# Meta keys' row maxima taken off by one product of 16 rows instead of eight with diagonals, in layer 0's attention

## What is computed

```python
x = L0_attn_x
xn = _layernorm(x, axis=-1)
x = x + _L0_attn_ref(xn, ...) + _L0_ffn_ref(xn, ...)
xn = _layernorm(x, axis=-1)
x = x + _L1_attn_ref(xn, ...) + _L1_ffn_ref(xn, ...)

# in _L0_attn_ref: N_HEADS = 16, N_KV_HEADS = 4, WINDOW = 64, N_META = 16, hd = 16
for qs in range(0, S, WINDOW):
    k_c = jnp.concatenate([k[:, :, :meta_end], k[:, :, ls:qe]], axis=2)
    allowed = causal & (in_window | meta)
    scores = jnp.einsum('bhqd,bhkd->bhqk', q_c, k_c) * scale
    scores = jnp.where(allowed[None, None], scores, -jnp.inf)
    attn = jax.nn.softmax(scores, axis=-1)
    chunks.append(jnp.einsum('bhqk,bhkd->bhqd', attn, v_c))
```

## Time and profile before

| | |
|---|---|
| three runs | 1292.34, 1292.8, 1294.93 us (median 1292.8) |
| profiled execution, its own time | 1302.65 us |
| its span, first to last instruction | 1300.9 us |
| TensorE busy | 1243.3 us, 96% |
| VectorE busy | 706.2 us, 54% |
| ScalarE busy | 576.4 us, 44% |
| GpSimd busy | 728.1 us, 56% |
| mean granted TensorE clock | 0.984 |

### The profile page before, as it was taken

How to read it: one execution, slowest core, us unless ns; L and a number is a source line. 1 busy time by engine, 2 the same in 40 slices (tenths; PEclk the granted TensorE clock), 3 DMA queues, 4 the chain that set the end, 5 groups by cost and what they waited for, 6 DMA issues and landing times. The chain is left out here.

```text
span 1300.9 us, 22025 instructions
## 1 busy us (share of the span) xinstructions
PE 1243.3 (96%) x7969; PEld 1075.5 (83%) x7969; DVE 706.2 (54%) x1449; ACT 576.4 (44%) x1239; POOL 728.1 (56%) x549
## 2 busy tenths in 40 slices
PE   7688999999989998999999999999999999999999
PEld 6467888888857887888788888888888888899988
DVE  6994555555667667675645434434434334554445
ACT  4675566666555333334333334333343333444431
POOL 4646777776203554566666664766556554177620
PEclk9699999999998999999999999999999999999999
DMA  9624888876705111121221112111111102699931
GB/s 314 166 54 108 180 174 189 177 172 128 175 2 174 62 49 53 62 65 49 77 70 62 37 53 70 53 37 53 57 62 32 42 25 66 236 349 342 361 130 65
DMA packets 112698, 150.71 MB, mean 116 GB/s; under 512 B 12144, under 2 KB 94192, under 8 KB 112464
## 3 DMA queue, kind: packets, MB, share of 16 engines
q1 hardware_dynamic: 96320, 123.21, 29.8%
q0 software_dynamic: 16272, 26.10, 10.5%
HBM read 121.31 MB, written 27.97 MB: 115 GB/s over the span
## 5 line engine op out<-in xcount | busy, mean ns | idle before, releaser
L1679 PE MATMUL a_p_p<-a_xr,a_wr 128*128 128x512 f32 x1152 | 308.7, 403 | 2.4 <-DVE g_x L2239 2.4
L1679 PEld LDWEIGHTS a_p_p<-a_xr,a_wr 128*128 128x128 f32 x1152 | 206.6, 189 | 42.7 <-DVE g_x L2239 3.1
L2006 POOL TENSOR_TENSOR a_sqsum<-a_sqsum,a_sq 128x512 f32<-128x512 f32 x60 | 77.9, 1298 | 232.6 <-ACT a_sq L1888 232.6
L1974 POOL TENSOR_TENSOR a_wr<-g_hold,a_wr 128x768 fp32r<-128x768 f32 x63 | 122.1, 1938 | 19.9 <-DVE a_wr L2038 19.9
L2074 DVE SCALAR_TENSOR_TENSOR a_gated<-a_th,a_p_o 128x512 f32<-128x512 f32 x64 | 44.0, 688 | 159.2 <-ACT a_sq L1888 159.2
L412 POOL DMA_INDIRECT acc<-l_ye,g_slot_token x64 | 102.9, 1607 | 39.2 <-ACT l_ye L780 22.3
L2008 POOL TENSOR_TENSOR a_gr<-a_gated,a_gr 128x512 fp32r<-128x512 f32 x64 | 97.8, 1528 | 23.7 <-DVE a_gr L2078 23.7
L1692 PE MATMUL a_p_p<-a_wvr,a_xr 128*128 128x512 f32 x384 | 108.6, 421 | 0.8 <-DVE a_xr L2032 0.8
L1750 PE MATMUL a_p_w<-a_gr,l_wo_r 128*128 128x512 f32 x384 | 100.7, 397 | 0.3 <-POOL a_gr L2008 0.3
L1861 ACT ACTIVATE a_qk<-a_p_p 128x512 f32<-128x512 f32 x64 | 38.2, 597 | 140.9 <-PE a_p_p L1679 140.9
L1734 PE MATMUL a_p_o<-a_sc,a_v 128*128 128x128 f32 x512 | 90.0, 278 | 6.7 <-DVE a_sc L2054 6.7
(11 more groups left out here) (296 smaller groups left out, 2851.2 us busy)
## 6 DMA issues: line engine op xcount, KB each, us to landing
g_hold<-in_Wqkg SPq DMA_DIRECT2D x64, 384.0 KB, 3.1
e_up<-in_gate_up SPq DMA_DIRECT2D x23, 1024.0 KB
g_hold<-in_gate_up SPq DMA_DIRECT2D x64, 192.0 KB
e_down<-in_down SPq DMA_DIRECT2D x23, 512.0 KB, 5.8
g_hold<-in_Wv SPq DMA_DIRECT2D x16, 512.0 KB, 4.6
l_down<-in_down SPq DMA_DIRECT2D x64, 96.0 KB
acc<-l_zero SPq DMA_DIRECT2D x2, 2176.0 KB, 12.5
rows<-l_zero SPq DMA_DIRECT2D x1, 2955.5 KB, 27.3
```

The source lines that it names most:

```text
L1679: mm = pe.matmul(dst[:, :], wr[n % 2][:, wp, kk, c * P:(c + 1) * P], xr[n // H1 % 2][:, xp, kk, :], start=(kk, xp, wp) == (0, 0, 0), stop= ...
L1974: pool.tensor_tensor(wr[n % 2][:, 1, :, :], w[n % 2], wr[n % 2][:, 0, :, :], ALU.subtract).then_inc(w_parts, 1)
L2006: pool.tensor_tensor(sqsum[b % 2][:, :], sqsum[b % 2][:, :], sq[a % 2][:, :], ALU.add).then_inc(summed, 1)
```

## The change

The row maxima of a tile's four groups are now kept in one tile `tops` (128 queries x 16 heads) instead of one `top` per group. In the step of `turn_meta`, and ahead of `turn_scores`, TensorE transposes `tops` into the bank of `p_t` that the meta slot will use (`turn_tops`). VectorE multiplies that, 16 rows x 128 repeated four times, with a constant `head` that leaves in each of the four only the rows of the heads that belong there, and writes `meta_max`, 16 x 512 (`spread_tops`). `turn_meta` waits for that, computes the meta keys' scores in the same bank, and takes the maxima off by one product of `metas` (16 x 128, -1 where the row's key/value head is the head's) with `meta_max`. The constant `minus` shrinks from 1280 to 256 columns, and `metas` and `head` come in.

```diff
-        minus = m.sb("minus", [P, 2, G0 + 1, P], F32R)
+        minus = m.sb("minus", [P, 2, P], F32R)
+        metas = m.sb("metas", [H0, P], F32R)
+        head = m.sb("head", [H0, R0])
+        meta_max = [m.sb(f"meta_max{s}", [H0, R0, P], F32R) for s in range(2)]
-        top = [m.sb(f"top{s}", [P, R0]) for s in range(3)]
+        tops = [m.sb(f"top{s}", [P, H0]) for s in range(3)]
...
-            sp.dma_start(loaded[:, M1:M2], io["c_minus"]).then_inc(masks_in, 16)
+            sp.dma_start(loaded[:, M1:M1 + 2 * P], io["c_minus"]).then_inc(masks_in, 16)
+            sp.dma_start(metasf, io["c_metas"]).then_inc(masks_in, 16)
...
-            pool.tensor_copy(minus[:, :, :, :], minusf[:, :, :, :]).then_inc(rounded, 1)
+            pool.tensor_copy(minus[:, :, :], minusf[:, :, :]).then_inc(rounded, 1)
+            pool.tensor_copy(metas[:, :], metasf).then_inc(rounded, 1)
...
+            def turn_tops(t):
+                slot = SLOTS * t + G0
+                pe.wait_ge(exps_done, slot - 1)
+                pe.wait_ge(max_done, 2 * G0 * (t + 1))
+                pe.transpose(p_t[slot % 2][0:H0, 0, :], tops[t % 3][:, :], ident[:, :]).then_inc(tops_in_psum, 1)
 
             def turn_meta(t):
                 b, slot = t // TPB, SLOTS * t + G0
                 bank = p_t[slot % 2]
-                pe.wait_ge(exps_done, slot - 1)
+                pe.wait_ge(meta_ready, t + 1)
                 if t % TPB == 0:
                     pe.matmul(bank[:, :, :], identb[:, :], maskT[:, 2, :, :], start=True, stop=False, skip_group_check=True)
                 for a in range(2):
                     pe.matmul(bank[:, :, :], km[:, b, a, :], qT[t % 3][:, a, :, :], start=a == 0 and t % TPB > 0, stop=False,
                               skip_group_check=True)
-                for kv in range(G0):
-                    for h in range(2):
-                        mm = pe.matmul(bank[:, :, HALF * h:HALF * (h + 1)], minus[:, h, 1 + kv, :],
-                                       diag[(G0 * t + kv) % 6][:, :, :], start=False, stop=True, skip_group_check=True)
-                mm.then_inc(turned, 1)
+                pe.matmul(bank[:, :, :], metas[:, :], meta_max[t % 2][:, :, :], start=False, stop=True, skip_group_check=True)\
+                    .then_inc(turned, 1)
...
                 if 0 <= v < STEPS:
+                    if v % G0 == G0 - 1:
+                        turn_tops(v // G0)
                     turn_scores(v)
                     if v % G0 == G0 - 1:
                         turn_meta(v // G0)
...
+            def spread_tops(t):
+                dve.wait_ge(tops_in_psum, t + 1)
+                if t >= 2:
+                    dve.wait_ge(turned, SLOTS * (t - 1))
+                dve.tensor_tensor(meta_max[t % 2][:, :, :], p_t[(SLOTS * t + G0) % 2][0:H0, 0, :].unsqueeze(1).to_broadcast([H0, R0, P]),
+                                  head[:, :].unsqueeze(2).to_broadcast([H0, R0, P]), ALU.mult).then_inc(meta_ready, 1)
...
                 for k in ticks_at[n][0:1]:
                     tick(k)
+                if 0 <= v < STEPS and v % G0 == G0 - 1:
+                    spread_tops(v // G0)
```

More of the change, by code:

```diff
@@ L63, in layer0_constants @@
     minus = np.where(half, -1.0, 0.0) * np.ones((1, 1, P))
-    of_kv = np.arange(P)[None, :] // 32 == np.arange(G0)[:, None]
+    of_kv = np.arange(P)[None, :] // 32 == np.arange(H0)[:, None] // R0
+    head = np.arange(H0)[:, None] % R0 == np.arange(R0)[None, :]
     return {
@@ L68, in layer0_constants @@
         "c_maskT": np.concatenate([cols.reshape(P, 2 * P), metas], 1).astype(np.float32),
-        "c_minus": np.concatenate([minus[:, :, None, :], minus[:, :, None, :] * of_kv[None, None]], 2)
-            .reshape(P, 2 * (G0 + 1) * P).astype(np.float32),
+        "c_minus": minus.reshape(P, 2 * P).astype(np.float32),
+        "c_metas": np.where(of_kv, -1.0, 0.0).astype(np.float32),
+        "c_head": head.astype(np.float32),
         "c_eye2": np.tile(np.eye(HALF), (2, 1)).astype(np.float32),
@@ L217, in layer0 @@
         loaded = probs[:, :, :, :].rearrange("p s r q -> p (s r q)")
-        M0, M1, M2 = 2 * KEYS0, 2 * KEYS0 + 3 * P, 2 * KEYS0 + 3 * P + 2 * (G0 + 1) * P
+        M0, M1, M2 = 2 * KEYS0, 2 * KEYS0 + 3 * P, 2 * KEYS0 + 3 * P + 3 * P
         maskf = loaded[:, 0:M0].rearrange("p (a n) -> p a n", a=2)
         maskTf = loaded[:, M0:M1].rearrange("p (a n) -> p a n", a=3)
-        minusf = loaded[:, M1:M2].rearrange("p (a b n) -> p a b n", a=2, b=G0 + 1)
+        minusf = loaded[:, M1:M1 + 2 * P].rearrange("p (a n) -> p a n", a=2)
+        metasf = loaded[0:H0, M1 + 2 * P:M2]
         yTs = m.sb("yTs", [P, R0, P])
@@ L271, in layer0 @@
         block = stack.enter_context(nc.Block())
-        BLANK, ROUNDED = 8, 5
+        BLANK, ROUNDED = 8, 6
         kind = lambda t: min(t % TPB, 1)
@@ L305, in _ @@
             sp.dma_start(row[:, :], io["c_row"]).then_inc(consts_in, 16)
+            sp.dma_start(head[:, :], io["c_head"]).then_inc(consts_in, 16)
             sp.dma_start(flip[:, :], io["c_flip"]).then_inc(consts_in, 16)
@@ L391, in _ @@
                 if t == 1:
-                    pool.wait_ge(consts_in, 96)
+                    pool.wait_ge(consts_in, 112)
                 for i in range(3 * (t - 1), 3 * t):
@@ L537, in turn_scores @@
                 for h in range(2):
-                    mm = pe.matmul(bank[:, :, HALF * h:HALF * (h + 1)], minus[:, h, 0, :], diag[n % 6][:, :, :],
+                    mm = pe.matmul(bank[:, :, HALF * h:HALF * (h + 1)], minus[:, h, :], diag[n % 6][:, :, :],
                                    start=False, stop=True, skip_group_check=True)
                 mm.then_inc(turned, 1)
+            def turn_tops(t):
[3 more added lines that the diff above has]
+                pe.transpose(p_t[slot % 2][0:H0, 0, :], tops[t % 3][:, :], ident[:, :]).then_inc(tops_in_psum, 1)
             def turn_meta(t):
@@ L644, in _ @@
                 if n == 0:
-                    pe.wait_ge(consts_in, 96)
+                    pe.wait_ge(consts_in, 112)
                     pe.wait_ge(xT_kept, NT)
@@ L758, in diagonal @@
                 for r in range(R0):
[L759 removed]
+                    ins = act.activation(diag[n % 6][:, r, :], eye2[:, :], ACT.Copy, scale=tops[n // G0 % 3][:, R0 * (n % G0) + r:R0 * (n % G0) + r + 1])
                 ins.then_inc(act_diag, 1)
@@ L907, in select @@
                 if h == 0:
-                    dve.wait_ge(consts_in, 96)
+                    dve.wait_ge(consts_in, 112)
                 dve.scalar_tensor_tensor(chosen[:, :, h, :], rest[:, half, :], IS_TAKEN,
@@ L989, in maxima @@
                     dve.wait_ge(act_diag, n - 2)
+                top = tops[n // G0 % 3][:, R0 * (n % G0):R0 * (n % G0 + 1)]
                 for c in range(2):
@@ L992, in maxima @@
                     dve.wait_ge(scored, pp + 1)
-                    dve.tensor_reduce(top[n % 3][:, 2 * c:2 * c + 2], p_s[pp % 2][:, :, 0:KEYS0], AX_X, ALU.max).then_inc(max_done, 1)
+                    dve.tensor_reduce(top[:, 2 * c:2 * c + 2], p_s[pp % 2][:, :, 0:KEYS0], AX_X, ALU.max).then_inc(max_done, 1)
                 if n >= SCALED:
```

8 lines of the change are left out of this document (4 added, 4 removed).

## The result

The changed kernel takes 1316.62 us (median of four, 1312.69 to 1318.11) against 1292.8 us before: a ratio of 1.0162, interval 1.0139 to 1.0184. It is slower, as forecast, but by some 21 to 24 us rather than 10, and it lies outside the range of 1296 to 1309. The profiled execution took 1315.61 us with a span of 1313.8.

What follows compares the result with a forecast made beforehand. TensorE was taken to bound the kernel from 120 to 375 us, VectorE from 60 to 98. Tile delays of 2.2 + 4.4 + 3.45 = 10.0 us, added to the median 1292.8, gave 1302.8 us; range 1296.3 to 1309.

Steps and rivals of the forecast that it cites:

- the block behind the wait: TensorE's meta products and 16-row product up to `project_y`: 0.57 + 0.235 = 0.80 us after a wait.
- What bounds the kernel: TensorE from 120 to 375 us, where the windows show it nearly always busy; VectorE's picks from 60 to 98 us.
- TensorE's own work: Each of 16 tiles loses 0.95 us, gains a 0.235 us product and a 0.10 us transpose: 0.62 us less without waits.
- VectorE's product: VectorE's new multiplication of 16 partitions by 512 columns, one operand in PSUM, priced at 0.69 us.
- The new wait: Ahead of the first meta product TensorE waits for VectorE's product, 0.86 us in tile 6; `project_y` there 0.34 us later.
- Tiles with ticks: Tiles 3 to 10: each ends 0.05 to 0.57 us later, sum 2.2 us.
- my own formula: A tile's end is the end of VectorE's work ahead of its new product, plus 1.49 us.
- Tiles without ticks: Tiles 11 to 15: each ends 0.70 to 1.28 us later, sum 4.4 us.
- ScalarE's list is the same: Part of the rest, which was put at nothing: ScalarE's work doesn't change.
- The three early tiles: Tiles 0 to 2: 1.23, 1.43 and 0.79 us later, sum 3.45 us.
- the clock falls: Rival: TensorE drops from 2.4 to 1.2 GHz behind waits in tiles 0 to 3 and 11 to 15, losing another 4 to 8 us; chance 0.08.
- the wait is hidden: Rival: VectorE's product is done before TensorE is through `turn_scores`, so 9.9 us are saved, 1282.9 us; chance 0.07.

Runs made afterwards that it cites:

- e9_before_wait: The kernel before the change, with only TensorE's wait for ScalarE's exp moved ahead of `turn_scores` in each tile's last step; ratio 1.0032 to the kernel before.
- e6_full_rows: The changed kernel with its 16-row product made a product of 128 rows, zero from row 16 on, same waits and order; ratio 1.0080 to the kernel before.
- e7_lag_full: The changed kernel with the meta slot one step later and the 16-row product made one of 128 rows; ratio 0.9973 to the kernel before.
- the control: The kernel before the change, nothing altered, profiled again and timed against itself; ratio 1.0002 (0.9984 to 1.0020).
- e11_fill_waits: The changed kernel with two useless products in each of TensorE's two new waits in tiles 0 and 1; ratio 1.0124 to the kernel before.
- e2_early_spread: The changed kernel with the transpose right behind `score` and VectorE's product right behind the maxima; ratio 1.0087 to the kernel before.
- e8_lag_middle: The changed kernel with meta slot one step later and 128 rows in tiles 3 to 12 only, the old way elsewhere; ratio 0.9950 to the kernel before.
- e3_filler: The changed kernel with four useless products ahead of `score` in steps 5 to 10; ratio 1.0194 to the kernel before.
- e4_old_first: The changed kernel with tiles 0 to 2 done in the old way, eight products with diagonals; ratio 1.0092 to the kernel before.
- e5_lag: The changed kernel with the meta slot, including ScalarE's exp of it, moved one step later; ratio 1.0023 to the kernel before.
- e1_no_shift: The changed kernel without transposes and VectorE's 16 products; the 16-row product multiplies zeros, so meta scores aren't shifted; ratio 0.9953 to the kernel before.

## Why the prediction was wrong in size

The direction was right, and so was the wait that it rests on. Two steps failed. The prediction kept TensorE's clock at 1.00 and gave its fall a chance of 0.08; the fall cost some 8 of the 11.8 us by which the layer's end missed the forecast (21.8 late against 10.0). And it priced the block behind the wait at 0.80 us, which measured 1.10.

**What bounds the kernel: right in the middle and at the end.** Idle time added to TensorE's list came out as time. For 60 to 98 us I had written that VectorE's picks set the pace; `e9_before_wait` adds nothing to VectorE, only a wait to TensorE, and is 2.9 us late by tile 1, so TensorE counts there as well.

**TensorE's own work: right for the eight products and the transpose, wrong for the product of 16 rows.** I gave the bounds 0.12 to 0.235 us, on the ground that the number of columns is the same. It takes 0.42 to 0.43 (L566 to L599), after a delay of its own: 0.67 instead of 0.57 from L564 to L566. The step that failed here is "its bounds are 0.12 us and 0.235 us", and with it the block behind the wait: 0.80 forecast, 1.10 measured, and 0.1 more inside `project_y`. `e6_full_rows` and `e7_lag_full` show that the 16 rows are the cause and the wait is not. The Trainium skill (TensorE: Matmul & The Clock Gate, "LDWEIGHTS (loading the stationary operand)") states that a load's time goes by its columns, not by its rows. The duration of the load agrees: 181 ns with 16 rows, 188 with 128. What differs is when it begins, which is seen in the loader's idle time ahead of it and not in its duration. Why it doesn't start under the product before isn't shown. Only 16 and 128 rows were tried for this product; that the tick's loads of 96 rows begin under the product before says that it isn't any number below 128.

**VectorE's product: right,** 0.672 for 0.69.

**The new wait: right in place.** TensorE waits for VectorE in all 16 tiles. In tile 6 the wait is shorter than forecast: `turn_scores` starts at 209.97 and takes 0.69 us, so TensorE is ready at 210.66, and it starts at 211.28, 0.62 us instead of 0.86. VectorE's product begins a little before the row ahead has ended (210.56 against 210.63), which I had not counted, and that row ends earlier beside TensorE's list than in the profile I used.

**Tiles with ticks: 3.3 us measured in tiles 4 to 10, some 2.05 forecast.** Two terms were mis-sized, in opposite directions, and the forecast came as near as it did partly by luck. One is the block: with 128 rows the same stretch loses 0.5 us. The other is how late VectorE is. In the profile before, L1045 ends between 0.01 us ahead of the first meta product's start and 0.50 us behind it, from tile to tile; I took this scatter for the kernel's own. In the control it ends 0.04 to 0.09 us behind it in each of these tiles. Tile 6 of the control:

```profile
197.15 0.28 DVE L1045 TENSOR_TENSOR l_hT<-l_th,l_p_e 96x128 f32<-96x128 f32 x1
197.34 0.62 PE L549 MATMUL l_p_t<-l_qT,l_km 128*128 128x512 f32 x2
198.77 1.03 PE L587 MATMUL l_p_y<-l_wo,l_yT 128*128 128x256 f32 x4
```

By my own formula that is 197.43 + 1.49 = 198.92 against 198.77, 0.15 us, and 0.8 us for tiles 4 to 10 together instead of 2.05. To this the block adds 0.4 us in each of seven tiles (0.3, and 0.1 in `project_y`), 2.8 us: 3.6, against 3.3 measured.

**Tiles without ticks: 6.3 us, 4.4 forecast.** Tiles 11 to 15 of the change lose 1.09, 1.06, 1.05, 1.63 and 1.30 us on the control, where I had 0.72, 0.72, 0.70, 1.28 and 0.97. Each is 0.33 to 0.37 more, which is what the block was too small by. The wait for ScalarE ahead of `turn_scores` was in no step. In the timeline of tile 14 of the change it is 1.13 us:

```profile
379.69 0.28 PE L555 MATMUL l_p_t<-g_ident,l_top 128*16 128x128 f32 x1 [1.13 <-ACT l_probs L766]
```

I had written that "ScalarE's list is the same", which is true, and looked no further at where TensorE now waits for it. Here it adds nothing to be seen in the sum: VectorE's list runs on beside it without idle time until its product ends at 381.60, and TensorE's L564 waits another 0.99 us for that. In `e9_before_wait`, where no wait for VectorE lies behind it, it costs time.

**The three early tiles: 12.2 us up to tile 3, 3.6 forecast (tile 3's 0.15 included).** Some 8 us are the clock (`e11_fill_waits`). Counted from TensorE's start behind the 2.19 us of idle time, the change is 11.3 us late at tile 3 and `e11_fill_waits`, with TensorE kept at work in the waits, 3.1, close to the forecast. Of the two new waits, that for ScalarE alone costs 2.2 up to tile 3 (`e9_before_wait`), with the clock at 0.78 from 67 to 82 us.

**The rival "the clock falls"** had 0.08, and against it I put that TensorE had been idle for 6.3 of 38 us at a clock of 1.00. The control shows how thin that was: the unchanged kernel, run again, has 0.93 from 67 to 82 us, with a fall that is over by 70 us (1.00 in the windows of 3 us from 70 to 121 us). The first profile shows no fall there, the control does, with the same 2.19 us of idle time ahead: the kernel stood at the edge, and in the change the new waits come within 4 us behind a fall. I had also placed the rival's cost at 4 to 8 us and spread it over the end of the layer as well as its start; some 8 us fell at the start alone, and at the end the change's profile has none.

**The rival "the wait is hidden"** names the right condition (VectorE free 0.69 us earlier). `e2_early_spread` meets it in tiles with ticks, and there a tile becomes 0.34 us shorter than in the control. Not 0.62, since the 16-row product still costs what it costs; with 128 rows and the wait gone (`e8_lag_middle`) it is 0.60.

**The profile's own time.** That I added the shift to the median and not to the profiled 1302.65 was right: 5 of those 9.9 us were lost in one place, between tiles 2 and 3, and the control's profile took 1296.89. But I still used that profile's rows for how late VectorE is.

What stays open: why the clock falls late in layer 0, somewhere from 355 to 390 us, in some kernels and not in others. `e2_early_spread`, `e3_filler`, `e4_old_first`, `e5_lag`, `e6_full_rows`, `e7_lag_full`, `e9_before_wait` and `e11_fill_waits` have such a fall; the change, `e1_no_shift` and `e8_lag_middle` have not. No run told these apart, and with one profile of each kernel the differences between places behind tile 12 hold this fall as well.

## What to carry to other kernels

Fewer instructions on the full engine pay only if what they need is ready without a new wait: before counting the saving, list the waits that the new order moves ahead of work that used to run first, those for engines the change doesn't touch too. Where the granted clock dips anywhere near, cost an added wait at the low level as well, and profile the unchanged kernel twice: it shows whether the clock stands at the edge, and which differences from tile to tile belong to the kernel and which to that one execution. The product with 16 rows wasn't cheaper than its neighbours, it cost nearly twice as much; look at the loader's idle time ahead of such a product, and try the full 128 rows with zeros.

## What the runs showed of the hardware

- In a stream of products with 128 rows, one of 16 rows (512 columns) takes 0.42 us to the next, one of 128 rows 0.23 us. Its load (181 ns) begins only when the product before is nearly done (0.36 to 0.4 us of idle time of the loader), and the next load of 128 rows isn't hidden under it either (0.25 us). Loads of 96 rows in the same stream begin under the product before.
- Behind the same 2.19 us without work in the first tiles, TensorE's granted clock stayed at 1.00 in the first profile of the kernel before and fell to 0.50 in the control and in the change. In the control it was back by 70 us; in the change, with two more waits of 0.80 and 0.51 us soon behind, it stayed low until some 77 us, and was low again from 88 to 98. With work without use in these waits (`e11_fill_waits`) it was back by 70 us and stayed at 1.00 until tile 10 and beyond.
